# Audio tower with attention and eight experts: expert outputs split by sequence, the last fold on POOL, queries and keys earlier in TensorE's order

## The reference

```python
# tokens: 248 windows of 8 positions, each weighed and projected to 64 columns
out = einsum('blfd,fd,fdk->blk', windows, filt, W);  h = relu(out + b_k)
# attention, one head of 64, on layernorm(h); rows with q[0]==0 or k[0]==0 are masked
scores = einsum('bid,bjd->bij', q, k) / 8;  prob = softmax(where(mask, scores, -1e9))
h = h + (prob @ v) @ Wo.T + bo
# mixture of 8 experts on x = layernorm(h): the top 2 of 8 gate logits, softmax over the two
combine = one_hot(topk_idx) * topk_w, summed over the two      # tokens x 8
y_e = relu(x @ W1[e] + b1[e]) @ W2[e] + b2[e]                   # hidden size 128
h = h + sum_e combine[:, e] * y_e
```

## Time and profile before

| | |
|---|---|
| profiled execution | 308.53 us, its span 306.7 us |
| mean granted TensorE clock | 0.967 of full speed |
| PE busy | 285.2 us (93%), 1486 matmul records |
| PEld busy | 190.7 us (62%) |
| DVE busy | 230.6 us (75%), 824 instructions |
| ACT busy | 234.2 us (76%), 545 |
| POOL busy | 99.0 us (32%), 85 |
| DMA | 28.61 MB in 17,247 packets, 13,760 of them of 512 B to 2 KB |
| chain of waits | PE 70%; of it `bank_y` (expert output) 15% of the span |

### The profile page before, as it was taken

How to read it: one execution, slowest core, us unless ns; L and a number is a source line. 1 busy time by engine, 2 the same in 40 slices (tenths; PEclk the granted TensorE clock), 3 DMA queues, 4 the chain that set the end, 5 groups by cost and what they waited for, 6 DMA issues and landing times.

```text
span 306.7 us, 5597 instructions
## 1 busy us (share of the span) xinstructions
PE 285.2 (93%) x1486; PEld 190.7 (62%) x1486; DVE 230.6 (75%) x824; ACT 234.2 (76%) x545; POOL 99.0 (32%) x85
## 2 busy tenths in 40 slices
PE   8767979999999999999999999999999998989882
PEld 8545556767585767666666758576766665545330
DVE  2577395878888797978697878879797889794543
ACT  2356577988979898988888797989898889776460
POOL 2112121162434343242416243434324232323113
PEclk9989589999999999999999999999999999999797
DMA  6511106153252617080615244251706061516060
GB/s 175 151 32 35 35 18 153 33 136 69 86 136 66 156 43 176 21 198 5 176 44 168 55 115 106 86 135 29 192 20 165 4 151 36 149 36 153 1 168 17
DMA packets 17247, 28.61 MB, mean 93 GB/s; under 512 B 3264, under 2 KB 13760, under 8 KB 17216
## 3 DMA queue, kind: packets, MB, share of 16 engines
q1 hardware_dynamic: 16928, 27.98, 36.4%
q10 hardware_dynamic: 288, 0.28, 0.3%
HBM read 21.90 MB, written 2.29 MB: 79 GB/s over the span
## 4 chain that ended last, share of the span: by engine, by line
PE 70%; DVE 9%; DMA 8%; issue 4%; ACT 3%; SPq 3%; POOL 1%; POOLq 0%; DVEq 0%; ACTq 0%
PE bank_y L887 15%; PE bank_a L827 11%; PE bank_h L877 8%; PE bank_h L878 7%; PE bank_s L936 4%; PE bank_s L855 4%; DMA cb<-weights 4%; PE bank_s L844 4%; PE bank_s L892 3%; PE bank_b L892 2%; PE bank_s L896 2%; PE bank_s L956 2%; PE bank_b L896 2%; DMA weights<-ct_sb 2%; PE bank_s L919 2%
## 5 line engine op out<-in xcount | busy, mean ns | idle before, releaser
L381 ACT ACTIVATE hid<-bank_h,col 128x496 f32<-128x496 f32 x128 | 82.9, 674 | 24.7 <-PE bank_h L878 23.7
L332 POOL TENSOR_TENSOR p<-p,rmask 124x496 f32<-124x496 f32 x32 | 35.6, 1111 | 97.1 <-DVE rmask L587 96.4
L887 PE MATMUL bank_y<-hid,w_sb 128*64 128x496 f32 x256 | 64.1, 601 | 0.2 <-ACT hid L381 0.2
L877 PE MATMUL bank_h<-xs,w_hi 128*128 128x496 f32 x128 | 58.1, 454 | 2.4 <-ACT hid L381 1.6
L569 DVE SCALAR_TENSOR_TENSOR acc<-bank_y,col,cb 128x496 f32<-128x496 f32 x64 | 44.9, 725 | 8.3 <-DMA cb<-weights 3.4
L878 PE MATMUL bank_h<-xs,w_lo 128*128 128x496 f32 x128 | 50.3, 393 | 0.0
L339 POOL TENSOR_TENSOR x_lo<-x,x_hi 128x512 fp32r<-128x512 f32 x16 | 20.6, 1288 | 56.7 <-ACT x_hi L437 56.7
L256 POOL TENSOR_TENSOR total<-acc 128x496 f32<-128x496 f32 x16 | 20.0, 1251 | 41.0 <-DVE acc L569 41.0
L372 ACT ACTIVATE p<-bank_s,nmax 124x248 f32<-124x248 f32 x64 | 29.0, 463 | 2.4 <-DVE nmax L576 1.7
L887 PEld LDWEIGHTS bank_y<-hid,w_sb 128*64 128x64 f32 x256 | 15.9, 138 | 22.7 <-issue 14.6
L877 PEld LDWEIGHTS bank_h<-xs,w_hi 128*128 128x128 f32 x128 | 24.7, 193 | 8.0 <-ACT hid L381 3.1
(11 more groups left out here) (105 smaller groups left out, 550.0 us busy)
## 6 DMA issues: line engine op xcount, KB each, us to landing
cb<-weights SPq DMA_DIRECT2D x64, 248.0 KB, 4.7
kk<-kk SPq DMA_DIRECT2D x16, 248.0 KB, 2.9
x<-xt SPq DMA_DIRECT2D x15, 256.0 KB, 2.8
out<-h SPq DMA_DIRECT2D x16, 124.0 KB, 1.8
w_sb<-w SPq DMA_DIRECT2D x3, 256.0 KB, 3.9
wtok_sb<-wtok SPq DMA_DIRECT2D x1, 256.0 KB, 2.7
x<-xt ACTq DMA_DIRECT2D x1, 256.0 KB, 3.8
weights<-ct_sb SPq DMA_DIRECT2D x16, 15.5 KB, 1.4
```

The costliest lines, as they stand in the source:

```text
L332: pool.tensor_tensor(p_sb[b][0:HALF, :, :], p_sb[b][0:HALF, :, :], rmask[0:HALF, b, :].unsqueeze(2).to_broadcast([HALF, 2, WIN]), ALU.mult ...
L381: act.activation(hid[2 * (p % 2) + s][:, :], bank_h[s][:, 0:TOK], ACT.Relu, bias=col[:, C_B1 + e:C_B1 + e + 1]).then_inc(hid_ready[s], 1)
L877: pe.matmul(bank_h[e % 2][:, 0:TOK], w1_hi[:, e, :], xs[m % 2][:, :], start=True, stop=False)
L887: last = pe.matmul(bank_y[p % 2][s * D:s * D + D, 0:TOK], w2_sb[:, 2 * p + s, :], hid[2 * (p % 2) + s][:, :], start=True, stop=True)
```

## The change

- `expert_out` writes sequence b of the group to half b of the partitions, and expert s of the pair to half s of the columns of `bank_y`. A pair is four matmuls of 248 columns in place of two of 496.
- `cb` is `[128, 8, 248]` in place of `[128, 4, 496]`; the layout of the weights in SBUF and DRAM and the biases' columns match it. `weigh` is two instructions of 248 columns per pair.
- `total` then needs its two column halves added. POOL's new `fold_halves` does it, one addition of 128x248 into `both`; PE's `fold_halves` and its constant are gone; `final` reads `both`.
- In all lists calls change place. Where a call moves across the end of an iteration, it handles the group by its next letter there (the `d` of one iteration is the `c` of the next).

ACT: before, ... relu 0, 1 | later_taps | relu 2 | turned 0, 1 | relu 3 | high_queries | high_keys | high_inputs | rectify | square | relu 4 ...; after, ... relu 0, 1 | turned 0 | relu 2 | later_taps | turned 1 | relu 3 | high_queries | high_keys | high_inputs | square | relu 4 | rectify ..., and `gate_exp` behind `relu` 7. The rest of the diff (left out are the host's layouts):

```diff
 cw2 = sb("cw2", [128, CHUNKS, EXPERTS])
-cw = sb("cw", [128, EXPERTS, CHUNKS])
+cw = sb("cw", [128, PAIR, EXPERTS, 2])
 ct_sb = sb("ct_sb", [CHUNKS * EXPERTS, HALF])
-cb = sb("cb", [128, EPAIRS, TOK])
+cb = sb("cb", [128, EXPERTS, WIN])
 hid = [sb(f"hid{i}", [128, TOK]) for i in range(4)]
...
 total = sb("total", [128, TOK])
+both = sb("both", [128, WIN])
...
-        after(eng, fin_done, m)
+        after(eng, fold_ready, m)
         eng.tensor_tensor(total[:, :], acc[0][:, :], acc[1][:, :], ALU.add).then_inc(sum_ready, 1)
...
             after_hold(sp, cb_in[half], 32 * m)
-        sp.dma_start(weights_dram.rearrange("e (j t) -> (e j) t", j=CHUNKS),
+        sp.dma_start(weights_dram.rearrange("b e (i t) -> (b e i) t", i=2),
                      ct_sb[:, :]).then_inc(ct_stored, 16)
...
     def spread(m, half):
...
         for s in range(2):
-            src = weights_dram.rearrange("(p s) t -> s p t", s=2)[s:s + 1, 2 * half:2 * half + 2, :]
-            sp.dma_start(cb[s * D:s * D + D, 2 * half:2 * half + 2, :],
-                         src.to_broadcast([D, 2, TOK])).then_inc(cb_in[half], 16)
+            src = weights_dram[s:s + 1, 4 * half:4 * half + 4, :]
+            sp.dma_start(cb[s * D:s * D + D, 4 * half:4 * half + 4, :],
+                         src.to_broadcast([D, 4, WIN])).then_inc(cb_in[half], 16)
...
     def load(d):
...
     def iteration(t):
-        d, c, n, m = t, t - 1, t - 2, t - 3
+        d, n, m = t, t - 2, t - 3
+        if live(m):
+            spread(m, 1)
+        if live(n):
+            store_weights(n)
+            spread(n, 0)
         if live(t + 3):
...
                 load(t + 3)
-        if live(n):
-            spread(n, 0)
-            spread(n, 1)
         if live(d):
             copy_keys(d)
-        if live(c):
-            store_weights(c)
         if live(m):
...
+    def fold_halves(f):
+        pool.wait_ge(sum_ready, 3 * f + 3)
+        after(pool, out_ready, f)
+        pool.tensor_tensor(both[:, :], total[:, 0:WIN], total[:, WIN:TOK], ALU.add).then_inc(fold_ready, 1)
     def low_inputs(d):
...
     def iteration(t):
-        a, c, m = t + 1, t - 1, t - 3
-        if live(a):
-            low_inputs(a)
-        if live(m):
-            add(pool, m, 1)
-        if live(c):
-            scale(c, 0)
-            scale(c, 1)
+        d, n, m = t, t - 2, t - 3
         if live(m):
             add(pool, m, 2)
+            fold_halves(m)
+        if live(t + 2):
+            low_inputs(t + 2)
+        if live(n):
+            add(pool, n, 1)
+        if live(d):
+            scale(d, 0)
+            scale(d, 1)
...
         after(dve, sum_ready, 3 * m + (-1, 0, 1, 1)[p])
-        dve.scalar_tensor_tensor(out=acc[p % 2][:, :], in0=bank_y[p % 2][:, 0:TOK],
-                                 scalar=col[:, C_B2 + p:C_B2 + p + 1], in1=cb[:, p, :], op0=ALU.add,
-                                 op1=ALU.mult).then_inc(acc_ready, 1)
+        for s in range(2):
+            e, half = 2 * p + s, slice(s * WIN, (s + 1) * WIN)
+            last = dve.scalar_tensor_tensor(out=acc[p % 2][:, half], in0=bank_y[p % 2][:, half],
+                                            scalar=col[:, C_B2 + e:C_B2 + e + 1], in1=cb[:, e, :], op0=ALU.add,
+                                            op1=ALU.mult)
+        last.then_inc(acc_ready, 1)
...
     def rowmax(n, b):
...
         after(dve, ct_done, m)
-        dve.tensor_tensor(cw[T, :, :].rearrange("p e j -> p j e"), cw1[T, :, :], cw2[T, :, :],
+        dve.tensor_tensor(cw[T, :, :, :].rearrange("p b e i -> p b i e"),
+                          cw1[T, :, :].rearrange("p (b i) e -> p b i e", b=PAIR),
+                          cw2[T, :, :].rearrange("p (b i) e -> p b i e", b=PAIR),
                           ALU.add).then_inc(topk, 1)
...
     def both_taps(c):
...
     def final(f):
...
-        dve.wait_ge(fin_done, f + 1)
-        dve.tensor_tensor(h2[f % 3][:, :], bank_s[1][:, 0:WIN], h2[f % 3][:, :], ALU.add).then_inc(out_ready, 1)
+        dve.wait_ge(fold_ready, f + 1)
+        dve.tensor_tensor(h2[f % 3][:, :], both[:, :], h2[f % 3][:, :], ALU.add).then_inc(out_ready, 1)
...
         after(pe, ct_ready, m)
-        pe.transpose(bank_b[0:CHUNKS * EXPERTS, 0:HALF], cw[0:HALF, :, :].rearrange("p e j -> p (e j)"),
+        pe.transpose(bank_b[0:CHUNKS * EXPERTS, 0:HALF], cw[0:HALF, :, :, :].rearrange("p b e i -> p (b e i)"),
                      ident[0:HALF, 0:HALF]).then_inc(ct_done, 1)
...
     def hidden(m, e):
...
         for s in range(2):
-            last = pe.matmul(bank_y[p % 2][s * D:s * D + D, 0:TOK], w2_sb[:, 2 * p + s, :],
-                             hid[2 * (p % 2) + s][:, :], start=True, stop=True)
+            for b in range(PAIR):
+                last = pe.matmul(bank_y[p % 2][b * D:b * D + D, s * WIN:(s + 1) * WIN], w2_sb[:, 2 * p + s, :],
+                                 hid[2 * (p % 2) + s][:, b * WIN:(b + 1) * WIN], start=True, stop=True)
         last.then_inc(y_done, 1)
...
     def centre(g, which, dst, src):
...
-    def fold_halves(f):
-        pe.wait_ge(sum_ready, 3 * f + 3)
-        pe.wait_ge(pt_ready, 2 * bounded(f + 3))
-        if f + 2 >= GROUPS:
-            pe.wait_ge(out_ready, f)
-        for b in range(PAIR):
-            last = pe.matmul(bank_s[1][b * D:b * D + D, 0:WIN], fold, total[:, b * WIN:(b + 1) * WIN],
-                             start=True, stop=True)
-        last.then_inc(fin_done, 1)
     def first_centre(c):
...
         after(pe, pt_ready, 2 * c)
-        after(pe, out_ready, c - 2)
         for i in range(2):
...
```

More of the change, by code:

```diff
@@ L95, in audio_tower @@
         meanof = cst[:, K_MEAN:K_MEAN + 128]
-        fold = cst[:, K_FOLD:K_FOLD + D]
         x_sb = [sb(f"x{i}", [128, PAIR, LEN]) for i in range(2)]
@@ L501, in iteration @@
                     relu(n, 1)
+                if live(c):
+                    turned(c, 0)
+                if live(n):
+                    relu(n, 2)
                 if live(a):
                     later_taps(a)
+                if live(c):
+                    turned(c, 1)
                 if live(n):
-                    relu(n, 2)
-                if live(c):
-                    turned(c, 0)
+                    relu(n, 3)
             run(iteration)
@@ L759, in iteration @@
                 if live(n):
-                    weights(n)
+                    one_hot(n)
                 if live(d):
@@ L765, in iteration @@
                 if live(n):
-                    both_weights(n)
-                    low_tokens_2(n, 1)
+                    weights(n)
                 if live(c):
@@ L789, in iteration @@
                         attention_parameters()
-                if live(m):
-                    add(dve, m, 3)
                 if live(c):
@@ L794, in iteration @@
                 if live(m):
-                    final(m)
+                    add(dve, m, 3)
                 if live(d):
@@ L800, in iteration @@
                         expert_parameters()
+                    keep_values(d)
+                    masks(d)
+                if live(m):
+                    final(m)
+                if live(c):
+                    normalise_2(c)
                 if live(n):
                     weigh(n, 0)
-                    weigh(n, 1)
+                if live(c):
+                    logits(c)
+                    low_tokens_2(c, 0)
+                    largest(c)
+                    low_tokens_2(c, 1)
             run(iteration)
@@ L976, in iteration @@
                 a, d, c, n, m = t + 1, t, t - 1, t - 2, t - 3
+                if live(m):
+                    hidden(m, 2)
+                    hidden(m, 3)
+                if live(c):
+                    if c == 0:
+                        parameter_products()
+                    queries_keys(c)
+                if live(n):
+                    turn_p(n, 1)
+                if live(m):
+                    expert_out(m, 0)
+                if live(n):
+                    attend(n)
+                if live(m):
+                    expert_out(m, 1)
+                if live(n):
+                    second_centre(n)
+                if live(m):
+                    hidden(m, 4)
+                if live(c):
+                    values(c)
+                if live(n):
+                    variance(n, 1, bank_s[0])
                 if live(a):
@@ L979, in iteration @@
                 if live(m):
[L980 to L982 removed]
+                    hidden(m, 5)
                 if live(d):
                     first_centre(d)
[L985 to L990 removed]
                 if live(a):
@@ L994, in iteration @@
                     gate(n)
+                if live(m):
+                    hidden(m, 6)
                 if live(d):
@@ L998, in iteration @@
                     conv(a, range(4, 6))
-                if live(c):
-                    scores(c, 0)
                 if live(m):
@@ L1003, in iteration @@
                 if live(c):
+                    scores(c, 0)
                     scores(c, 1)
```

(5 more changed lines are left out.)

83 lines of the change are left out of this document (22 added, 61 removed).

## The result

Over 14 runs each on the same chip the changed kernel takes a median of 306.43 us (305.65 to 308.16) and the kernel before 308.00 us (306.34 to 309.65): ratio 0.9945, interval 0.9923 to 0.9968. That is 0.55% faster, within the 1% that the prediction called no change, and 0.7 us beside its 307.1. The profiled execution took 306.96 us, its span 304.3 us.

The account below looks back on a forecast made before the run. PE, working end to end in a clean iteration, was taken to bound the kernel. 308.53 - 4.7 (fold) + 5.0 (new waits) - 1.45 (late DMAs) - 0.3 (ends) = 307.1 us; range 302 to 312.

Parts of the forecast that it names:

- Fold: PE's fold goes to POOL: 0.43 us less in each of eleven iterations, -4.7 us; POOL's addition taken at 0.7.
- Second transposes: PE waits 0.30 us an iteration for POOL's second softmax product: 2.67 us from the combine weights' transpose against PE's 2.37.
- Gate and attention product: PE waits per iteration: 0.08 us ahead of the gate (bounds 0, 0.3), 0.07 at the attention product (0, 0.2).
- Queries and keys early: On PE, ahead of the second transposes: worth little to PE, since what they feed keeps its room before the scores.
- Weight loads: Expert output: 16 more an iteration at 0.138 us each, costed at nothing, covered by the neighbouring column half.
- rival 2: Expert output's added weight loads come into the open: 1.1 us an iteration, 14.3 in all, 321 us; chance 0.10.
- `final` "counted unchanged": DVE's `final` reads SBUF in place of PSUM, keeps its shape and is costed at no change.
- DMAs: Late DMAs over the eleven iterations, 1.45 us in all, disappear: -1.45 us, bounds 0 and -1.45.
- rival 1: The waits do not form, at most 0.1 of 0.45 us an iteration left: 4.6 us less, 302.5; chance 0.28.
- rival 3: DVE becomes the bound at the gate: wait 0.53 instead of 0.08 us, 5.9 in all, 313 us; chance 0.12.
- Signs: Clean iterations 16.4 to 16.5 us; second transposes' weight loads idle about 0.3; no row of weighing waiting for combine weights.
- Ends: Outside the eleven full iterations: -0.3 us together, including -0.65 for the last group's first half of the weights alone.

Follow-up runs that it names:

- turn_earlier: Changed kernel with PE's hidden(n, 1) moved behind turn_weights(n): 302.36 us, ratio 0.9827 to the kernel before.
- recip_first: Changed kernel with DVE's masked_recip(c, 1) moved directly behind recip(c, 1), ahead of the combine weights' copy: 309.07 us, ratio 1.0025 to the kernel before.
- queries_late: Changed kernel with PE's queries_keys(c) put back behind the second transposes, turn_p(n, 1): 312.38 us, ratio 1.0124 to the kernel before.
- same_half: Changed kernel with expert_out's two loops exchanged, so neighbouring matmuls use the same column half: 306.98 us in a single run.
- split_only: Kernel before with expert output split by sequence and fold on POOL behind its second sum, all lists in old order: 330.56 us, ratio 1.0719.
- split_sp_order: Kernel before with split, POOL fold, `final` behind low_keys, second low tokens ahead of fourth weighing, SP's new list: 310.11 us, ratio 1.0074.

## Why the prediction was right

The number was right, and so was the main mechanism: the fold leaves PE, and most of what that frees is spent on a new wait at the second transposes. But how close the number came is in part luck. The eleven iterations gained twice what I forecast, 1.1 us more, and 1.0 of it came back outside them, most of that outside the span, where I had no term.

| step | predicted | measured |
|---|---|---|
| an iteration without fold and waits | 16.03 | 16.04 (turn_earlier) |
| wait at the second transposes | 0.30 | 0.24, and 0.05 in the transposes |
| wait at the gate | 0.08 | 0 |
| wait at the attention product | 0.07 | 0 |
| clean iteration | 16.48 | 16.33 |
| late DMAs over eleven iterations | none left of 1.45 | 0.66 left (180.29 - 11 x 16.33) |
| eleven iterations | -1.15 | -2.28 |
| span outside them | -0.3 | -0.1 |
| execution less span | unchanged | +0.83 |
| sum | -1.4 | -1.57 |

- **Fold.** Its 0.43 us did leave PE. POOL's addition took 0.72, where I had taken 0.7 between 0.6 and 1.25, and was done at 182.68, 1.5 us before `final`.
- **Second transposes.** The new wait formed where it was predicted, on the path that was predicted: 2.60 us from the transpose against 2.67. recip_first moved this wait, queries_late lengthened it by 0.45, turn_earlier removed it, and only the last made the kernel faster.
- **Gate and attention product.** Both waits were differences of long sums of spacings. Measured, the gate follows without a gap, and ScalarE's copy ended at 179.56, in time for expert pair 0 to last 0.99 in the chain, as before (0.98). A difference of 0.08 between two sums of ten terms is not a wait that can be read ahead.
- **Queries and keys early "are worth little to PE".** This reason failed, though the sum had it right: it counted their 0.46 inside PE's 2.37. They fill the wait; queries_late prices them at 0.45 us an iteration, some 6 us in all.
- **Weight loads.** Nothing came into the open (rival 2 is out), but I named the neighbouring column half as the cover, and none is needed: the full-width load of 0.19 us beside a hidden layer's record (183.85) is as hidden, and the order of the halves is worth 0.04 us for eight records (same_half). The rule of the Trainium skill that the prediction weighed against this (page "TensorE: Matmul & The Clock Gate", Part 3, The mechanism) would have added 1.1 us an iteration; no row here bears it out.
- **`final` "counted unchanged".** It was, 0.41 us, but not for the reason given. With both operands in SBUF it is held up when it starts beside a POOL instruction: 1.39 us in split_only. In the new order it starts 0.27 us after POOL's low inputs end (183.92 to 184.19). The price that I set at nothing hung on that place in the list.
- **DMAs.** In the eleven iterations the combine weights come in time (landing 3.9 us against 4.7); the key copy was late twice. The term was too hopeful by 0.66.
- **Rivals 1 and 3.** Two of rival 1's three waits did vanish, but the third stayed, and its 302.5 us is what turn_earlier reaches (302.36) once that wait has work in it. DVE never bound PE at the gate.
- **Signs.** Two of the signs that I named for myself misled. Clean iterations were to last 16.4 to 16.5 us and last 16.33. And the forecast was to be wrong if PE's busy share stayed at 99% of an iteration, since then 16.04 would hold: it stayed at 99.5% (179.36 of 180.29), yet the wait was there and the iteration lasts 16.33, because a record's modelled end hides the gap. The busy share doesn't show this wait of 0.24 us. The sign that held is the weight load of the second transposes, idle for 0.50 us behind POOL's product (at 194.61).
- **Ends.** The part ahead of the eleven iterations is 1.1 us shorter, that behind them 1.0 longer. The 0.65 that I gave the last group for sending its first half of the weights alone did not come: its weighing starts 4.60 us after that issue (290.21 to 294.81), against 4.70 before (292.76 to 297.46), and DVE waits 2.27 of them, a row that I had said would not be there. The shorter start goes with a granted clock of 0.90 in the first 50 us against 0.86, and so may belong to the run; that was not tested. The time outside the span is 2.2 us in the median of the changed kernel's runs (1.8 to 2.9) and 1.8 in nearly every run of the kernel before; why, no run shows.

Neither half of the change gains by itself: the new computation in the old lists costs 7.2%, the new lists with a fold on PE 7.4%, together they gain 0.55%. But both prices belong to single places in a list. With two DVE calls and SP's list moved the new computation loses only 0.7%, and the 7.4% hang on where PE's fold stands. How much each wait weighs in these two was read from their traces. An experiment with POOL's products on another engine, which would settle what the blocking costs the changed kernel itself, wasn't tried.

## What to carry to other kernels

Work that is taken off the busiest engine is worth only what the next late input lets through: find that input's origin, compare starts rather than brackets, and put independent work of the same engine between origin and use (here one call moved gained some 4 us, where the whole change had gained 1.6). When an engine takes over an operation or an operand moves from PSUM to SBUF, read what the engine that shares its SBUF access does at that very moment; a cost of nothing there is a property of the order, not of the instruction.

## What the runs showed of the hardware

- **DVE and POOL hold each other up, and 0.1 us can decide.** A DVE addition or product that reads two operands in SBUF and starts while a POOL instruction runs lasts until that ends, or up to 0.3 longer: 124x2 elements 0.79 instead of 0.16 us, 64x248 1.42 instead of 0.41, 128x248 1.39 instead of 0.41. How far POOL has got doesn't matter (`final` in split_sp_order starts some 0.9 us behind and still lasts 0.68), and in none of the twelve traces does one end ahead of the POOL instruction. In the changed kernel low keys and values, which read one operand in PSUM, take 0.74 and 0.43 beside POOL's low inputs (182.64 to 183.92), no more than elsewhere. The other way round, POOL's product of 124x496 takes 1.24 instead of 1.01 where DVE's low tokens start 0.05 us ahead of it, and 1.01 again in recip_first, where they don't. The Trainium skill has the cause (page "SBUF — State Buffer", section "SBUF: two separate sides"): the two share a port pair as an exclusive lock, which whoever starts first keeps for the whole instruction, DVE's with two SBUF inputs among them. The trace agrees for the two additions and the masked reciprocal; of POOL's product it shows 0.23 us more, where the low tokens ran on for 0.36 (193.32 to 193.68). DVE instructions with one tensor input differ. The key mask (0.57 in the mean in split_sp_order, 0.17 in the changed kernel) is held up too, so two inputs aren't needed; the plain reciprocal is not, with 0.17 us from 191.36 beside POOL's product from 191.29.
- **Float32 matmuls on the two halves of the array's width run side by side.** Eight records of 248 columns take 0.84 us, two per 0.21, which is what one such record takes on the full width. With two neighbouring matmuls in the same half, eight take 0.88.
- **Weight loads hide behind the matmul ahead** on half the width (0.138 us within 0.21) and on the full width (0.19 within 0.23), all of them with all 128 rows.
